# A two-layer decoder on one core: the last layers' entry loads moved into the expert layer, its gathers ordered by tile, one power call per norm

## The reference, cut to what matters

```python
x = _layernorm(x + _L0_attn_ref(x, ...))            # 16 heads of 64, causal
x = _layernorm(x + _L0_xattn_ref(x, ctx, mask, ...))
x = _layernorm(x + _L0_ffn_ref(x, ...))             # 8 experts, top 2: the expert layer
x = _layernorm(x + _L1_attn_ref(x, ...))            # gated attention with its MLP
x = _layernorm(x + _L1_xattn_ref(x, ctx, ctx, ...))
x = _layernorm(x + _L1_ffn_ref(x, ...))

def _layernorm(x, eps=1e-5):
    return (x - mean(x)) / sqrt(var(x) + eps)
```

## Time and profile before

| what | value |
|---|---|
| median of three runs | 1316.02 us |
| the profiled execution, its own time | 1315.13 us |
| its span in the trace | 1313.1 us |
| PE / DVE / ACT / POOL busy | 1121.8 / 738.3 / 537.9 / 454.8 us |
| TensorE's granted clock, mean | 0.949 |

### The profile page before, as it was taken

The page is one execution under the profiler, slowest core; times in us unless marked ns, Lnnn a source line. Parts: engine busy times, 40 slices in busy tenths (PEclk is TensorE's granted clock), DMA queues, the critical chain, the costliest instruction groups (busy, mean ns, idle before and its releaser), DMA issues. The chain is left out here.

```text
span 1313.1 us, 20231 instructions
## 1 busy us (share of the span) xinstructions
PE 1121.8 (85%) x6714; PEld 786.2 (60%) x6714; DVE 738.3 (56%) x2210; ACT 537.9 (41%) x1385; POOL 454.8 (35%) x548
## 2 busy tenths in 40 slices
PE   7889988997898886899999734776997899899996
PEld 3456456545644665899999712543664575467775
DVE  1472476248435825465555427657549676846366
ACT  1371255217323711333333125464465556534541
POOL 0150034005201576666666343224132522222022
PEclk9999999999999997899999957698998999899999
DMA  5000200020001040811111170001000100000000
GB/s 190 17 1 1 55 17 1 0 55 17 1 0 55 1 158 17 301 49 50 50 49 49 34 229 8 25 1 30 3 9 1 32 2 24 1 1 25 0 1 32
DMA packets 40226, 52.37 MB, mean 40 GB/s; under 512 B 10780, under 2 KB 33372, under 8 KB 40124
## 3 DMA queue, kind: packets, MB, share of 16 engines
q1 hardware_dynamic: 31100, 36.66, 8.8%
q0 software_dynamic: 3408, 9.31, 2.5%
q10 hardware_dynamic: 5616, 5.11, 1.2%
HBM read 41.76 MB, written 9.31 MB: 39 GB/s over the span
## 5 line engine op out<-in xcount | busy, mean ns | idle before, releaser
L1281 PE MATMUL bank<-words 128*128 128x256 f32 (+3 forms) x848 | 275.4, 476 | 31.7 <-ACT words L1792 17.3
L1281 PEld LDWEIGHTS bank<-words 128*128 128x128 f32 (+1 forms) x848 | 159.7, 195 | 122.0 <-issue 66.9
L358 PE MATMUL bank<-words 128*128 128x512 f32 x384 | 173.1, 602 | 8.3 <-DMA words<-in_wq 8.3
L324 POOL TENSOR_TENSOR words<-words 128x256 f32<-128x256 f32 (+1 forms) x128 | 103.6, 831 | 190.5 <-DVE words L700 190.5
L876 PEld LDWEIGHTS bank<-words 128*128 128x128 f32 x1248 | 147.7, 194 | 4.2 <-ACT words L910 2.3
L876 PE MATMUL bank<-words 128*128 128x128 f32 x1248 | 148.2, 278 | 1.6 <-ACT words L910 1.6
L571 ACT ACTIVATE words<-words 128x128 f32<-128x128 f32 (+1 forms) x256 | 113.3, 444 | 50.2 <-DVE words L695 50.2
L358 PEld LDWEIGHTS bank<-words 128*128 128x128 f32 x384 | 72.5, 193 | 90.6 <-issue 90.0
L553 ACT ACTIVATE words<-bank 128x512 f32<-128x512 f32 x48 | 28.7, 598 | 192.5 <-PE bank L358 192.5
L925 ACT ACTIVATE words<-words 128x1024 f32 x39 | 41.2, 1057 | 146.4 <-PE bank L876 113.1
L610 DVE COPY words<-bank 128x512 f32<-128x512 f32 x48 | 33.2, 691 | 106.2 <-PE bank L358 105.9
(11 more groups left out here) (263 smaller groups left out, 2035.5 us busy)
## 6 DMA issues: line engine op xcount, KB each, us to landing
words<-in_w SPq DMA_DIRECT2D x8, 1024.0 KB
y_slots<-words ACTq DMA_DIRECT2D x39, 128.0 KB
words<-in_w SPq DMA_DIRECT2D x8, 512.0 KB
words<-in_xt SPq DMA_DIRECT2D x4, 512.0 KB, 3.8
words<-in_x SPq DMA_DIRECT2D x4, 512.0 KB, 4.2
x_rows<-words SPq DMA_DIRECT2D x16, 128.0 KB
words<-in_wm SPq DMA_DIRECT2D x2, 1024.0 KB, 6.5
out_x<-words SPq DMA_DIRECT2D x16, 128.0 KB, 1.8
```

Of the source, the lines that this page charges most:

```text
L324: last = pool.tensor_tensor(part, part, inv[:, j % SLOTS0, :, t:t + 1].to_broadcast([P, 2, P * (t + 1)]), ALU.mult)
L358: last = pe.matmul(bank[c % 2][:, :], w, r, start=k == 0, stop=k == KD - 1)
L1281: last = pe.matmul(out, w, r, start=i == 0, stop=i == len(pairs) - 1)
```

## The change

Five edits.

1. The ten entry loads of the last layers (their constants and first weights) are issued by SyncE at the end of its part of `expert_layer`, into 6016 words a partition at the end of SBUF that the expert layer does not use. The index copy for group 0 and the constants -0.5 and eps are also made there, by GpSimd, after its last product; then it drains. The expert layer's block is opened with `no_gpsimd_drain=True`, so that GpSimd does not drain at its end.
2. The gathers of all groups go by tile: first and second choice of tile 0, then of tile 1, and so on. For group 0 VectorE combines in this order.
3. The two powers of n3 and n4 become one: VectorE prepares both arguments with four small operations behind the statistics, and GpSimd makes one power over a strided pair. This holds for all groups.
4. For groups 0 and 1 statistics, power and normalising are done by halves (two tiles each); groups 2 and 3 as a whole.
5. `const` comes later: GpSimd fills its constants after group 0's powers, and clears `va` only after the four tiles of group 0 are normalised. The waits for `const` move behind group 0's transposes on TensorE and ScalarE.

```diff
 # expert_layer
-        block = ctx.enter_context(nc.Block())
+        block = ctx.enter_context(nc.Block(no_gpsimd_drain=True))
 # its sync part, behind the expert loads
+            for name in ("bm1", "cols", "rope", "parity"):
+                part = keep["l_" + name]
+                sp.dma_start(part[...], dram[name]).then_inc(keep["rows"], 16)
+            sp.dma_start(keep["l_brow"][:, :, :], ...to_broadcast([P, 3, D])).then_inc(keep["rows"], 16)
+            for name in ("wgate", "wclock", "wpp", "wqk", "wv1"):
+                sp.dma_start(keep["l_" + name][:, :, :], ...).then_inc(keep["early"], 16)
 # its gpsimd part, behind the last product and before the waits for the stores
+            pool.tensor_copy(keep["l_at"][:, :, :], keep["slot"][:, :, 0:NT])
+            pool.memset(keep["l_minus_half"][:, :, :], -0.5)
+            pool.memset(keep["l_eps"][:, :], EPS)
+            pool.drain()
 # last_layers: sync (the ten loads go)
-            sp.wait_ge(n3.stats, 1)
+            sp.wait_ge(n3.stats, 2)
 # gpsimd
-                pool.tensor_copy(at[:, :, :], keep["slot"][:, :, bass.ts(g, NT)])
-                pool.drain()
-                for n in range(2 * NT):
+                if g > 0:
+                    pool.tensor_copy(at[:, :, :], keep["slot"][:, :, bass.ts(g, NT)])
+                    pool.drain()
+                for n in (r * NT + t for t in range(NT) for r in range(2)):
                     pool.indirect_dma_start(back[:, n, :], ...).then_inc(backed[n], 16)
...
+            def constants():
+                pool.memset(ones[:, :], 1.0)      # and tiny, mask1, maskx, x5t
+                pool.wait_ge(n3.normed, NT)
+                pool.memset(va[:, :, :, :], 0.0)
+                pool.drain()
+                pool.memset(va[:, :, :, DH1:DH1 + 1], 1.0)
+                pool.affine_select(out=mask1[:, :], ...)
+                pool.affine_select(out=maskx[:, :], ...)
+                pool.drain()
+                pool.nop().then_inc(const, 1)
-            def front_rstd(g):
-                norm_rstd(pool, g, n3, eps[:, :], minus_half[:, :])
-                ...                                  # three small operations
-                pool.tensor_tensor(n4.inv[:, :], n4.var[:, :], minus_half[:, :], ALU.pow).then_inc(n4.rstd, 1)
-            front_rstd(0)
+            def front_rstd(g, b=None):
+                h = tiles_of(b)
+                pool.wait_ge(n3.stats, front_count(g, b))
+                pool.tensor_tensor(powers[:, 2:4, h], powers[:, 0:2, h], minus_half[:, 2:4, h], ALU.pow).then_inc(n3.rstd, 1)
+            front_rstd(0, 0)
+            front_rstd(0, 1)
+            constants()
 # tensor
-            pe.wait_ge(const, 1)
             turn_front(0)
+            pe.wait_ge(const, 1)
 # scalar: the same; and a wait for each tile's half in front_rows
-                act.wait_ge(n4.rstd, g + 1)
                 for t in range(NT):
+                    act.wait_ge(n3.rstd, front_count(g, t // HALF))
 # vector
+            def front_half(g, b=None):
+                h = tiles_of(b)
+                ...                                  # bn_stats and bn_aggr of the tiles of h, as before
+                dve.drain()
+                dve.tensor_scalar(powers[:, 0, h], n3.mv[:, h, 1], EPS, None, ALU.add)
+                dve.drain()
+                dve.reciprocal(powers[:, 1, h], powers[:, 0, h])
+                dve.drain()
+                dve.tensor_tensor(powers[:, 1, h], n3.mv[:, h, 1], powers[:, 1, h], ALU.mult)
+                dve.drain()
+                dve.tensor_scalar(powers[:, 1, h], powers[:, 1, h], EPS, None, ALU.add).then_inc(n3.stats, 1)
+            def front_statistics(g):
+                for b in range(2) if g < 2 else (None,):
+                    front_half(g, b)
-            for n in range(2 * NT):
-                combine(0, n)
-            front_statistics(0)
-            dve.wait_ge(const, 1)
-            normalise(0, n3, lambda t: x(0, t))
+            for t in range(HALF):
+                combine(0, t)
+                combine(0, NT + t)
+            front_half(0, 0)
+            combine(0, 2)
+            combine(0, NT + 2)
+            front_rows_of(0, 0)
+            combine(0, 3)
+            combine(0, NT + 3)
+            front_half(0, 1)
+            front_rows_of(0, 1)
+            dve.wait_ge(const, 1)
```

More of the change, by code:

```diff
@@ L817, in _ @@
                     load_expert(sp, dram, keep, e + EARLY)
+            for name in ("bm1", "cols", "rope", "parity"):
+                part = keep["l_" + name]
+                sp.dma_start(part[:, :] if name in ("bm1", "parity") else part[:, :, :], dram[name]).then_inc(keep["rows"], 16)
+            sp.dma_start(keep["l_brow"][:, :, :], dram["rows"].rearrange("(o r) n -> o r n", o=1).to_broadcast([P, 3, D])).then_inc(keep["rows"], 16)
+            for name in ("wgate", "wclock", "wpp", "wqk", "wv1"):
+                sp.dma_start(keep["l_" + name][:, :, :], dram[name].rearrange("(k p) n -> p k n", p=P)).then_inc(keep["early"], 16)
         @block.gpsimd
@@ L1000, in last_layers @@
         sem = memory.sem
-        wqk = sb([P, KD, 2 * D])
-        wv1, wgate, wpp, wclock, wout = (sb([P, KD, D]) for _ in range(5))
+        wqk, wv1, wgate, wpp, wclock = (keep["l_" + n] for n in ("wqk", "wv1", "wgate", "wpp", "wclock"))
+        wout = sb([P, KD, D])
         wm1, wm2 = sb([P, KD, M1]), sb([P, MC, D])
@@ L1052, in last_layers @@
         lastxr, lastxk, lastrl, lastrs = (cut(gating, 1024 * i, dims) for i, dims in enumerate(((KD, GT), (KD, GT), (KD, GT), (NT, D))))
-        early, weights, rows, loaded, const, stored = (sem(f"l_{n}") for n in ("early", "weights", "rows", "loaded", "const", "stored"))
+        early, rows = keep["early"], keep["rows"]
+        weights, loaded, const, stored = (sem(f"l_{n}") for n in ("weights", "loaded", "const", "stored"))
         backed = [sem(f"backed{n}") for n in range(2 * NT)]
@@ L1103, in both, with tiles_of, front_count @@
             return bank[n][:, :].rearrange("p (c n) -> p c n", c=2)
+        def tiles_of(b):
+            return slice(0, NT) if b is None else slice(HALF * b, HALF * b + HALF)
+        def front_count(g, b):
+            return 2 * g + (b or 0) + 1 if g < 2 else g + 3
         def stages(p):
@@ L1233, in _ @@
                     if a + 1 < G:
-                        front_rstd(a + 1)
+                        if a == 0:
+                            front_rstd(1, 0)
+                            front_rstd(1, 1)
+                        else:
+                            front_rstd(a + 1)
                 if r is not None:
@@ L1880, in _ @@
             front_turned(0, 1)
+            act.wait_ge(const, 1)
             for p in range(PERIODS):
@@ L1914, in _ @@
                 if a is not None:
-                    powers(a, 5)
+                    p_rows(a, 5)
                 if r is not None:
@@ L2494, in decoder @@
         keep["behind"] = memory.mark
+        memory.mark = Memory.WORDS - 6016
+        for name, shape in (("wqk", [P, KD, 2 * D]), ("wv1", [P, KD, D]), ("wgate", [P, KD, D]), ("wpp", [P, KD, D]), ("wclock", [P, KD, D]),
+                            ("bm1", [P, MC]), ("cols", [P, 9, KD]), ("rope", [P, 2, 3 * DH1 // 2]), ("parity", [P, 2]), ("brow", [P, 3, D])):
+            keep["l_" + name] = memory.take(shape)
+        keep["l_minus_half"], keep["l_eps"] = memory.take([P, 4, NT]), memory.take([P, NT])
+        keep["l_at"], keep["l_rows_in"] = memory.take([P, 2, NT], I32), memory.take([P, 2 * 1024])
+        assert memory.mark <= Memory.WORDS
         keep["expload"] = [memory.sem(f"expload{n}") for n in range(EARLY)]
         keep["b1load"] = memory.sem("b1load")
+        keep["early"], keep["rows"] = memory.sem("l_early"), memory.sem("l_rows")
         memory.mark = first
@@ L2500, in decoder @@
         keep["cleared"] = memory.used[kept:]
-        memory.mark = keep["behind"]
+        memory.mark, memory.limit = keep["behind"], Memory.WORDS - 6016
         expert_layer(nc, dram, memory, keep)
```

84 lines of the change are left out of this document (36 added, 48 removed).

## The result

| what | before | after |
|---|---|---|
| median of nine runs each, us | 1315.58 | 1310.81 (1307.29 to 1313.39) |
| ratio, with its 95% interval | | 0.9964 [0.9949, 0.9978] |
| the profiled execution, its own time | 1315.13 | 1309.96 |
| its span | 1313.1 | 1308.2 |

The account below looks back on a forecast made before the run. The bound was taken to be bare latency at the entry of the last layers, before TensorE's first form. Entry -5.2, group 1 -0.5, period 1 +1.0, period 2 +0.1 sum to -4.6 us: 1316.02 to 1311.4, range 1307.0 to 1315.8.

Parts of the forecast that it names:

- The drain: End of the expert layer: GpSimd's early copy and drain, hidden by the stores, bring the first gather 3.5 us sooner.
- "debt" rival: The early drain does not clear its cost; the drain in the constants takes 3.26, not 0.7: 1314.0 us, chance 0.10.
- The loads: Ten entry loads moved into the expert layer: priced at nothing there, at worst 1.3 us.
- Gathers and the port: Entry: combinations beside gather issues cost 0.5 us in sum; rival, all six cost 0.5 each: 1313.9 us, chance 0.10.
- Half by half: Group 0 at the entry: powers and normalising by two tiles; fourth tile normalised at 769.3, form possible at 771.9.
- const holds TensorE for 0.9: Entry: const comes at 772.8 and delays TensorE by 0.9 us; first form at 772.9, 5.2 sooner than before.
- Group 1: Statistics to ScalarE's last scaling, done by halves: 0.5 us gained, bounds 0 and 1.
- Period 1: Four small operations and an eight-column power delay normalising and the next score pair: 1.0 us lost, bounds 0 and 1.4.
- Period 2: Two more VectorE operations before normalising make its pair 0.5 late: 0.1 us lost, at most 0.5.
- likeliest case: The forecast itself: 1311.4 us for the median, own range 1309.5 to 1313.3, chance 0.50.
- "clock falls well" rival: One half-clock stretch after the entry falls away, worth 2.15 us, and gathers are not delayed: 1308.8 us, chance 0.22.
- slower rival: Waiting in periods 1 and 2 drops the clock; four half-clock stretches cost 8.6 us: 1320.0 us, chance 0.08.

Follow-up runs that it names:

- 17 runs: All runs of the unedited changed kernel from two comparisons with the kernel before, taken together: 3.9 us [2.7, 4.9] below it by the means.
- second comparison: The changed kernel run once more, nothing edited, beside the kernel before: median 1311.68 us, ratio 0.9968 [0.9957, 0.9979].

## Why the prediction was right, point by point

- *The drain*: right. Forecast 3.5 for drain and copy; from the product's end to the first gather it went from 9.96 to 6.35, 3.6. The rule of 0.08 a gather was read from two drains; four more confirm it, and the "debt" rival is out (0.8 behind the value rows, not 3.3).
- *The loads*: right. They cost nothing where they are. Of the entry's 5.9 the loads alone give 1.4 and the drain 3.1; the copy's 0.5 leaves 0.9 for order by tile, halves and the single power, `const` being in the way. That is a difference, not a test: no kernel had these three alone.
- *Gathers and the port*: mis-sized, and the port misread. 0.5 was charged for combinations beside gather issues; seven of the eight took 0.95 and the first 1.02, so it is nothing here. Most of the 0.7 by which the entry beat the forecast is this term: the first power started 16.15 behind the product's end, 16.9 were forecast. The 1.28 on average from which I took the 0.5 was mostly the plain pitch of 1.25, its 0.30 between issues included; the rest was the first issue and one gather of 1.11, the only one of that entry that began under a combination. Here the same two, from the kernel before, and then the first power in the kernel after:

```profile
762.58 0.49 DVE L2110 SCALAR_TENSOR_TENSOR words<-words 128x256 f32<-128x256 f32 x1 [1.13 <-DMA words<-y_slots,words]
762.78 1.11 POOL L1156 DMA_INDIRECT words<-y_slots,words  x1 [0.30 <-issue]
```
```profile
760.81 0.48 DVE L2124 SCALAR_TENSOR_TENSOR words<-words 128x256 f32<-128x256 f32 x1
760.86 1.34 POOL L1208 TENSOR_TENSOR words<-words 128x4 f32<-128x4 f32 x1
```

  What decides is which begins first. In the change every combination beside the gathers begins at least 0.26 behind a gather's start, and costs nothing. The power began 0.05 behind a combination and took 1.34, where the second took 1.01. The prediction has all six combinations delay the gathers by the port's rule alone; it left this out, and the rival stayed away because of the order in time.
- *Half by half*: right to some tenths. The fourth tile was normalised 23.5 after the product's end (768.22), 24.1 were forecast: the 0.7 gained ahead of the first power, less what that power took longer.
- *const holds TensorE for 0.9*: right at the first form, 0.9 by the two kernels without the wait; at the end of the kernel the 0.9 was not seen. The sum has a slip: 769.3 and 3.4 make 772.7, not 772.8.
- *Group 1*: 0.5 forecast, 0.6 measured, but for the wrong reason in part: I worked it out by halves, and the whole group in one gives the same. The sum does not close either: two times 2.0 from 854.8 is 858.8, and 859.15 was written; by its own terms the gain would have been 0.9.
- *Period 1*: 1.0 forecast, 1.3 measured, and one pair sooner than I had put it. I had the long power delay the normalising and the last pair. In fact the four small operations delay the pair ahead of the normalising; its exponentials and the next scores are late by the same 1.32, and the wait for the power shrank behind that (0.59). The way that I had put is there too: the normalising ends at 949.35 and the pair of quad 7 starts at 949.38 without a wait, 4.91 behind the aggregation's start where it was 3.58. The scores that it needs end only 0.04 before it, so both ways bring the same 1.3. The step that failed is "with the four operations 953.8; power to 955.6": it priced the way to the power and left out the pair queued on VectorE behind the small operations. Their own price, 1.0, was right (0.97); the idle 0.35 before the third was in no term.
- *Period 2*: right. 0.1 forecast; TensorE's scores of quad 7 wait 0.16 in the kernel after and the pair runs at 1070.84 with no wait.
- *The clock*: the profiled execution after was ahead by 6.4 at the first form, by 9.2 at the first form of period 1 and by 4.8 at the last matmul. The waits explain -5.9, -0.6, +1.3 and +0.2 (period 2), in sum -5.0; the swings on top are stretches at 1.2 GHz that fall elsewhere. The likeliest case held, without the "clock falls well" rival. The slower rival did not come in the median; single executions can lose such an amount in part, as the 89.0 and 83.6 of one program show. By the means of 17 runs the gain is 3.9 [2.7, 4.9], below the 5.0 of the waits and at the edge of the interval; that the clock takes the difference is likely, as entries 1 to 2 us shorter were not seen at the end, but was not isolated.
- *The number*: that 4.8 came so near to 4.6 is in part luck. The entry was 0.7 better and period 1 0.3 worse than forecast, and the same program gave 4.3 by the medians of its second comparison and 3.9 by the means.

## What to carry to other kernels

Price a drain by the software DMAs issued since the last one and put it where something else is waited for anyway. When work is moved from one engine to another, price what is queued behind it on the new engine first, then the result's own way: here TensorE waited 1.3 us for four operations of 0.17. And where the clock of one program can shift a profiled execution by 5 us, read gains of 1 us from waits and from entry to entry, not from spans, and do not count them as time saved until the means show them. Ask of each pair on VectorE and GpSimd which begins first.

## What the runs showed of the hardware that was not expected

- A GpSimd drain takes 0.085 us for each gather issued since the last (3.26 behind 39, 1.8 behind 21, 1.5 behind 18, 0.05 behind none); the last of the 39 was issued some 14 us earlier.
- GpSimd's fills and its clearing of 2048 words, begun first, held two VectorE normalisings from 0.74 to 2.80. A gather that begins first is not held by a two-input combination, nor holds it (0.95 and 0.48, as alone); one that begins under such an operation is: 1.11 and 1.46, and a power of four columns took 1.34. Two gathers of the kernel before (823.32, 914.66) began 0.01 us after a `tensor_tensor` of VectorE had and took 0.95.
- GpSimd's power takes 0.70 for two columns, 1.01 to 1.05 for four where nothing held it, and 1.67 for eight.
- In one of two executions of one program TensorE stayed at 1.2 GHz for 47.8 us on end where the other had mean clock 0.71.
